# Second attention stage of a one-core graph network: the turn order of TensorE, ScalarE and VectorE rewritten

## The chip, the cores and the metric

The kernel runs on one core of one Trainium2 chip. The metric is the device time of one launch in microseconds (us); the time before is the median of three runs. A profile of one further execution was recorded.

## The reference, cut to what matters

A network of four graph layers over 100,000 nodes with 64 features and 50,000 edges, everything in float32. The change touches the second layer alone, a graph attention with four heads:

```python
h = jnp.maximum(_layernorm(x, axis=-1), 0.0)
xl = (h @ W_l + b_l).reshape(n, HEADS, C)
xr = (h @ W_r + b_r).reshape(n, HEADS, C)
e = (edge_attr @ W_e).reshape(-1, HEADS, C)
g = jax.nn.leaky_relu(xl[src] + xr[dst] + e, NEG_SLOPE)
logits = jnp.einsum('ehc,hc->eh', g, att)
amax = jax.ops.segment_max(logits, dst, num_segments=n)
ex = jnp.exp(logits - amax[dst])
denom = jax.ops.segment_sum(ex, dst, num_segments=n)
alpha = ex / (denom[dst] + 1e-16)
out = jax.ops.segment_sum(xl[src] * alpha[..., None], dst, num_segments=n).reshape(n, HEADS * C) + bias
mean, var = out.mean(axis=0), out.var(axis=0)
out = (out - mean) * jax.lax.rsqrt(var + BN_EPS) * gamma + beta
return jax.nn.gelu(out + h, approximate=False)
```

## The kernel before, in words

The kernel is a row of stages, one after the other, with a barrier between them; stage two is `conv_gatv2` (from L1366). Edges are sorted by target node and cut into 98 chunks of 512 edges. A chunk is worked on feature-major: a tile of 128 partitions by 512 columns holds the source node's 64 features in partitions 0 to 63 and the target's in 64 to 127.

Work is pipelined by hand. `slots` (L167) runs a body once per turn for every engine; in one turn the body gets the chunks k0, k1, ... k6, where k3 is the chunk that is three turns behind k0. Each engine runs the steps of its body in the order in which they are written, and semaphores tie the engines together; nothing else sets the order. The steps of one turn before the change are these.

- TensorE (body at L1543): the edge product `w_e1` into `p_g` (L1548) and the node product `w_lr` onto it (L1550), both for k3; the centering product of k2 (`norm.center`, L726); four transposes of the gathered rows of k0 (L1563); the variance product of k2 (L734); four transposes of the edge attributes of k2 (`ea.turn`, L1021); the score product of k3 (L1573); eight small products that add the finished rows of k6 to the column statistics (`stat.add`, L1046); four transposes of the running sums of k5 (L875).
- ScalarE (body at L1441): copy of the source half out of PSUM and of the position column for k1 (L1447, L1448); two activations that make `g` for k3 (L1454, L1455); the square of k2 (L730); the near exponential of k4 (L823); logarithm and exponential that make the reciprocal deviation of k2 (L741, L743); copy of the edge attributes of k2 (L1026); square of the finished rows of k6 (L1465); the far exponential of k4 (L828).
- VectorE (body at L1482): the normed and clamped tile `hT` of k3 (`norm.scale_to`, L748, a maximum with zero and a product in one instruction); the backward scan of k1 (L1494); then the softmax of k4, k5 and k6 interleaved: the denominator (L848), a carried column (L787), the scan of the sums (L837), the reciprocal (L852), the scan of the maxima (L806), the mask (L1513), near difference (L810), carried far sum (L814), quotient (L857), a copy of the mask for the statistics (L1525), far difference (L818), and last the weights (L1531).
- GpSimd gathers: per turn it copies the row numbers (L906) and issues four indirect transfers (L918), held until ScalarE's L1448 has freed a row buffer three turns on.
- SyncE issues seven transfers per turn (L1396 to L1419): target rows, a keep mask, the stores of `xT`, `hT` and the output rows, the far mask and the edge attributes; each is held by a semaphore of the step that fills or frees its buffer.

`p_cen` (the centered tile, PSUM) and the square have one buffer each, `xT` and `hT` four, `p_g` two. The edge attributes are transposed into the bank of the variance, `p_var`, so the variance product of a turn can come only when the attributes of the turn before have been copied out.

Of the kernel before, what the change touches and what calls it, by code (L numbers as in the profile page):

```python
# [31 lines left out]
P = 128  # L32
D = 64
TPC = 4
# [162 lines left out]
def hold(eng, sem, n):  # L197

    eng.wait_ge(sem, n)
    eng.nop(nofuse=True)  # L200
# [1165 lines left out]
def conv_gatv2(nc, c, dram, x1, e1, eo1, edge_attr, xs, hs):  # L1366
# [4 lines left out]
    with Scope(nc, "l1") as s:  # L1371
        rows = Rows(s, [(x1, POS + D, 0, c.idx_src)], POS + 2 * D)
        kept = Kept(s, 2 * D)
        norm = NormT(s, "n")
        sm = Softmax(s, 1)
        xT = [s.sb(f"xT{q}", [P, CE]) for q in range(4)]
        hT = [s.sb(f"hT{q}", [P, CE]) for q in range(4)]
        ea = EdgeAttr(s, edge_attr, 16, 0, norm.p_var)
        g = s.sb("g", [P, CE])
        keep = [s.sb(f"keep{u}", [P, CE]) for u in range(2)]  # L1380
        last = s.sb("last", [P, TPC])
        stat = Stats(s)
        end_rows, end_x, end_T = s.sb("end_rows", [P, POS + D]), s.sb("end_x", [P, P]), s.sb("end_T", [P, P])
        p_xT, p_score = s.ps("p_xT"), s.ps("p_score")
# [9 lines left out]
        with nc.Block() as block:  # L1394
# [40 lines left out]
            @block.scalar  # L1435
            def _(act):
                load_ln_exp(nc, act)
                act.wait_ge(end_gathered, 16)
                act.activation(c.end_pos[:], end_rows[:, 0:POS].bitcast(I32), ACT.Copy).then_inc(m["end_put"], 1)

                def body(k1, k2, k3, k4, k6):  # L1441
                    if k1:
                        if not k1.round:
                            act.wait_ge(x_saved[k1.q], 16 * k1.r)
                            act.wait_ge(norm.centered, k1.n - 4)
                        act.wait_ge(m["x_turned"], k1.n)
                        act.activation(xT[k1.q][0:D, :], p_xT[0:D, :], ACT.Copy).then_inc(m["src_out"], 1)  # L1447
                        act.activation(c.idx_pos[:, bass.ds(k1.i * TPC, TPC)].unsqueeze(2), rows.buf[k1.q][:, :, 0:POS].bitcast(I32),  # L1448
                                       ACT.Copy).then_inc(rows.rows_free, 1)
                    if k3:  # L1450
                        if not k3.start:
                            act.wait_ge(m["scored"], k3.n - 1)
                        act.wait_ge(m["g_summed"], k3.n)
                        act.activation(g[0:D, :], p_g[k3.u][0:D, :], ACT.Identity, bias=c.b_g1[0:D, 0:1])  # L1454
                        act.activation(g[D:P, :], p_g[k3.u][0:D, :], ACT.Relu, bias=c.b_g1[0:D, 0:1]).then_inc(m["g_ready"], 1)  # L1455
                    if k2:
                        norm.square(act, k2)
                    if k4:
                        sm.exp_near(act, k4.n)
                    if k2:  # L1460
                        norm.rsqrt(act, c, k2)
                        ea.copy_out(act, k2.n)
                    if k6:
                        act.wait_ge(kept.out_ready, k6.n)
                        act.activation(kept.out[k6.q][:, :, D:P], kept.out[k6.q][:, :, 0:D], ACT.Square).then_inc(m["sums_ready"], 1)  # L1465
                    if k4:
                        sm.exp_far(act, k4.n)
                slots(act, c.NCH, 6, lambda k0, k1, k2, k3, k4, k5, k6: body(k1, k2, k3, k4, k6))
                stat.scalar(act, c)

            @block.vector
            def _(dve):
# [6 lines left out]
                early(dve.tensor_copy(end_T[D:P, :], p_xT[D:P, 0:P]))  # L1479
                step = Steps(dve, m["even_step"], m["odd_step"])  # L1480

                def body(k1, k3, k4, k5, k6):  # L1482
                    if k3:
                        if not k3.round:
                            dve.wait_ge(h_saved[k3.q], 16 * k3.r)
                        if not k3.first:
                            dve.wait_ge(m["g_summed"], k3.n - 2)
                        norm.scale_to(dve, k3, hT[k3.q][:])
                    if k1:
                        if not k1.round:  # L1490
                            dve.wait_ge(x_saved[k1.q], 16 * k1.r)
# [26 lines left out]
                    if k6:  # L1518
                        if not k6.round:
                            dve.wait_ge(o_saved[k6.q], 16 * k6.r)  # L1520
                        if not k6.start:
                            dve.wait_ge(m["sums_added"], k6.n - 1)
                        step.ended(masked)
                        sm.quotient(dve, kept.out[k6.q][:, :, 0:D]).then_inc(kept.out_ready, 1)
                        dve.tensor_copy(last[:], c.last_d[:, bass.ds(k6.i * TPC, TPC)]).then_inc(m["last_ready"], 1)  # L1525
                    if k4:
                        step.ended(carried)
                        sm.shift_far(dve, k4)
                        dve.wait_ge(sm.near_exped, k4.n)
                        w = sm.weights()  # L1530
                        dve.scalar_tensor_tensor(w, p_g[k4.u][D:P, :], c.b_l1[D:P, 0:1], w, ALU.add, ALU.mult).then_inc(m["valued"], 1)  # L1531
                slots(dve, c.NCH, 6, lambda k0, k1, k2, k3, k4, k5, k6: body(k1, k3, k4, k5, k6), step)

                stat.vector(dve, c, c.gamma1, c.beta1, c.bias1, c.scale1, c.shift1, raw=True)

# [1 line left out]
            def _(pe):  # L1537
# [2 lines left out]
                pe.transpose(p_xT[:, 0:P], end_x[:], c.ident[:]).then_inc(m["end_turned"], 1)  # L1540
                hold(pe, m["early_step"], 3)

                def body(k0, k1, k2, k3, k4, k5, k6):  # L1543
                    if k3:
                        if not k3.first:
                            hold(pe, m["valued"], k3.n - 2)
                        hold(pe, ea.ready, k3.n)
                        pe.matmul(p_g[k3.u][:], c.w_e1[:].rearrange("p a f -> p (a f)"), ea.T[0][0:16, :], start=True, stop=False)  # L1548
                        hold(pe, norm.done, k3.n)
                        pe.matmul(p_g[k3.u][:], c.w_lr[:].rearrange("p a f -> p (a f)"), hT[k3.q][:], start=False, stop=True  # L1550
                                  ).then_inc(m["g_summed"], 1)
                    if k2:
                        hold(pe, m["src_out"], k2.n)
                        hold(pe, m["keep_used"], k2.n)
                        norm.center(pe, c, k2, xT[k2.q][:])
                    if k0:
                        if k1:
                            hold(pe, m["src_out"], k1.n)
# [4 lines left out]
                            ins = pe.transpose(p_xT[:, j * P:(j + 1) * P], rows.buf[k0.q][:, j, POS:POS + 2 * D], c.ident[:])  # L1563
                        ins.then_inc(m["x_turned"], 1)
                    if k2:
                        norm.variance(pe, c, k2)
                        hold(pe, norm.logged, k2.n)
                        ea.turn(pe, c, k2)
                    if k3:
                        if k4:  # L1570
                            hold(pe, sm.shifted, k4.n)
                        hold(pe, m["g_ready"], k3.n)
                        pe.matmul(p_score[:], c.w_att1[:], g[:], start=True, stop=True).then_inc(m["scored"], 1)  # L1573
                    if k6:
                        hold(pe, m["last_ready"], k6.n)
                        hold(pe, m["sums_ready"], k6.n)
                        stat.add(pe, last, kept.out[k6.q], m["sums_added"])
                    if k5:
                        if k6:
                            hold(pe, kept.out_ready, k6.n)  # L1580
                        sm.turn(pe, c, k5)
                slots(pe, c.NCH, 6, body)
                stat.finish(pe, c)


# [956 lines left out]
```

## Time and profile before

| what | value |
|---|---|
| median of three runs | 6815.02 us (6811.41 to 6820.18) |
| the profiled execution's own time | 6795.73 us |
| span of the profile | 6793.8 us |
| busy share of the span: TensorE, VectorE, ScalarE, GpSimd | 62%, 69%, 49%, 66% |
| mean granted TensorE clock | 0.895 of 2.4 GHz |
| products L1550 of stage two | from 1823.3 to 2812.0 us |

The sum of the prediction is made against the profiled execution. A timeline row gives the start, the duration, the engine (PE is TensorE, PEld its weight load, DVE VectorE, ACT ScalarE, POOL GpSimd, SPq the SyncE queue), the line, the operation and the tiles; x is the number of instructions merged into the row, and in brackets stands the idle time before it with what ended it. A row that covers two passes of one product (x2) gives them as one. Instructions of one engine can overlap by some hundredths of a microsecond, and TensorE's more, since its ends are modelled: distances from start to start are the safer reading.

### The profile page before, as it was taken

Reading aid. Unit: us, or ns where it says so; the run is one execution under the profiler, and the core shown is the slowest. Engines: PE = TensorE matmul, PEld = TensorE weight load, DVE = VectorE, ACT = ScalarE, POOL = GpSimd, SP = SyncE. Lnnn points to the kernel's source line nnn. Section 1 sums busy time; section 2 is a strip of 40 time slices with the busy share of each in tenths; the row PEclk is TensorE's granted clock in tenths of the full one; section 3 lists DMA queues with packets and bytes.
Section 4 is the critical chain, followed back from the end, with each engine's and each line's share of the span. In section 5 each row is a group of like instructions: output and inputs, shape, how many; then the busy total and the mean of one; then the engine's idle time right before and its main releaser. Section 6 shows DMA issues by size and latency. Waiting matters only on the chain. (4 is left out here: it accounts for less than half of the span.)

```text
span 6793.8 us, 85831 instructions
## 1 busy us (share of the span) xinstructions
PE 4193.3 (62%) x15111; PEld 2135.7 (31%) x15111; DVE 4701.1 (69%) x9073; ACT 3325.8 (49%) x5670; POOL 4502.1 (66%) x4877
## 2 busy tenths in 40 slices
PE   0102555555477777699996777775777677777700
PEld 0000211111133333266663333332434344444400
DVE  5885888888577777576664555555777667766667
ACT  1112444444355555487885666665777733333300
POOL 4777888888644444265546888886766477777744
PEclk9999999999999999799997888887999978778855
DMA  2442222222344444499983344443333233333377
GB/s 89 140 144 56 81 74 74 78 74 74 83 132 131 132 132 129 104 186 193 192 178 93 114 114 114 114 114 93 75 80 78 65 66 71 69 71 69 69 297 309
DMA packets 949964, 773.07 MB, mean 114 GB/s; under 512 B 661199, under 2 KB 727708, under 8 KB 945875
## 3 DMA queue, kind: packets, MB, share of 16 engines
q1 hardware_dynamic: 819859, 614.72, 30.6%
q0 software_dynamic: 125504, 131.83, 12.2%
q10 hardware_dynamic: 4512, 25.60, 0.9%
q14 instruction: 66, 0.54, 0.0%
q8 instruction: 23, 0.38, 0.0%
HBM read 472.43 MB, written 310.28 MB: 115 GB/s over the span
## 5 line engine op out<-in xcount | busy, mean ns | idle before, releaser
L205 ACT ACT_TABLE_LOAD x621 | 796.7, 1283 | 139.3 <-PEq L66 128.6
L954 POOL DMA_INDIRECT x<-l_out,l_snum x392 | 472.5, 1205 | 106.5 <-issue 90.1
L918 POOL DMA_INDIRECT l_rows<-x,l_num x392 | 441.2, 1126 | 153.5 <-issue 93.7
L954 POOL DMA_INDIRECT m<-l2s_out,l2s_snum x392 | 439.2, 1120 | 146.5 <-issue 105.7
L1159 POOL DMA_INDIRECT pre_src_rows<-in_x,all_idx_src x392 | 397.2, 1013 | 164.3 <-issue 130.0
L918 POOL DMA_INDIRECT l_rows<-in_x,l_num x392 | 432.1, 1102 | 105.7 <-issue 90.6
L918 POOL DMA_INDIRECT l3a_rows<-m,l3a_num x392 | 398.6, 1017 | 144.3 <-issue 93.3
L918 POOL DMA_INDIRECT l2s_rows<-vc_rows,l2s_num x392 | 416.5, 1062 | 106.3 <-issue 95.5
L918 POOL DMA_INDIRECT l_rows<-eo,l_num x392 | 387.5, 989 | 147.7 <-issue 96.7
L954 POOL DMA_INDIRECT xg<-l3b_out,l3b_snum x392 | 395.2, 1008 | 113.2 <-issue 90.3
L918 POOL DMA_INDIRECT l3b_rows<-g_rows,l3b_num x392 | 385.6, 984 | 106.2 <-issue 92.4
L837 DVE TENSOR_TENSOR_SCAN l2s_sums<-l2s_ex,l2s_sums 128x512 f32<-128x512 f32 x97 | 124.6, 1284 | 458.3 <-ACT l2s_ex L828 458.3
L1349 PE MATMUL l_p_hT<-all_ident,l_h 128*128 128x128 f32 x392 | 109.2, 433 | 468.5 <-DVE l_h L681 468.5
L2407 PE MATMUL l3b_p_gate<-all_w_gate,l3b_acc 128*128 128x256 f32 x784 | 305.4, 557 | 32.5 <-DVEq L2366 31.4
L310 ACT ACTIVATE prep_pay<-prep_pay 128x512 f32<-128x512 f32 x136 | 85.7, 630 | 416.9 <-DVEq L396 416.9
L734 PE MATMUL l_n_p_var<-l_n_sq,all_w_mean 128*128 128x512 f32 x392 | 220.7, 645 | 95.9 <-ACT l_n_sq L730 95.6
L2399 PE MATMUL l3b_p<-all_ident,l3b_hm 128*128 128x128 f32 x392 | 126.6, 345 | 231.0 <-DVEq L2359 231.0
L1349 PEld LDWEIGHTS l_p_hT<-all_ident,l_h 128*128 128x128 f32 x392 | 70.0, 217 | 631.6 <-DVE l_h L681 631.6
L432 PE MATMUL prep_ptk<-all_ident,prep_key 128*128 128x128 f32 x72 | 20.1, 434 | 402.2 <-DVEq L382 402.2
L1981 PE MATMUL l2s_p_score<-l2s_vT,all_w_head 68*128 68x512 f32 x196 | 110.3, 645 | 238.9 <-ACT l2s_vT L1918 238.9
L1708 DVE TENSOR_TENSOR_SCAN l_p_oT<-l_keep,l_end_T,l_p_oT 64x512 f32<-64x512 f32 x98 | 127.5, 1301 | 185.5 <-PE l_p_oT L1782 148.2
L2454 POOL TENSOR_TENSOR dl_min<-dl_min,all_shift 128x1600 f32<-128x1600 f32 x32 | 131.2, 4099 | 182.7 <-DMA dl_min<-m 182.7
(407 smaller groups left out, 13700.1 us busy)
## 6 DMA issues: line engine op xcount, KB each, us to landing
l_far<-far_d SPq DMA_DIRECT2D x196, 256.0 KB, 3.4
xg<-l2s_bg_row SPq DMA_DIRECT2D x97, 512.0 KB, 3.8
dl_xin<-xg SPq DMA_DIRECT2D x31, 1600.0 KB
l2s_bg_x<-x SPq DMA_DIRECT2D x97, 260.0 KB, 3.0
x<-ts_row SPq DMA_DIRECT2D x31, 812.5 KB, 4.4
l_keep<-keep_d SPq DMA_DIRECT2D x196, 128.0 KB, 2.9
xs<-l_xT SPq DMA_DIRECT2D x98, 256.0 KB, 2.7
hs<-l_hT SPq DMA_DIRECT2D x98, 256.0 KB, 3.0
```

Source lines behind the costliest of these rows:

```text
L205: act.add_instruction(mybir.InstLoadActFuncSet(name=nc.get_next_instruction_name(), ins=[], outs=[], act_func_set_id=which))
L734: pe.matmul(self.p_var[:], c.w_mean[:], self.sq[:], start=True, stop=True).then_inc(self.spread, 1)
L837: dve.tensor_tensor_scan(self.sums[k.u][:], self.ex[:, 0, :], self.ex[:, 1, :], 0.0 if k.start else self.sums[1 - k.u][:, CE - 1:CE], ALU. ...
L918: pool.indirect_dma_start(self.buf[k.q][:, j, at:at + w], None, table, bass.IndirectOffsetOnAxis(ap=self.num[k.q][:, m, j:j + 1], axis=0)) ...
L954: pool.indirect_dma_start(self.table, bass.IndirectOffsetOnAxis(ap=self.num[k.q][:, j:j + 1], axis=0), self.out[k.q][:, j, 0:self.cols], N ...
L1159: pool.indirect_dma_start(c.src_rows[:, t, :], None, x, bass.IndirectOffsetOnAxis(ap=c.idx_src[:, t:t + 1], axis=0)).then_inc(c.src_gather ...
L1349: ins = pe.transpose(p_hT[:, j * P:(j + 1) * P], h[:, j, :], c.ident[:])
L1708: swept = step(dve.tensor_tensor_scan(p_oT[D:P, ::-1], keep[k1.q][D:P, ::-1], p_oT[D:P, ::-1], end_T[D:P, bass.ds(k1.i, 1)], ALU.mult, ALU ...
L1981: pe.matmul(p_score[k1.u][:], c.w_head[:], vT[k1.u][:], start=True, stop=True).then_inc(m["scored"], 1)
L2399: pe.transpose(p_01[:, cols], hm[:, j, 0:P], c.ident[:])
L2407: ins = pe.matmul(p_gates[:, j, :], acc[k1.u][:, j * P:(j + 1) * P], c.w_gate[:], start=True, stop=True)
L2454: pool.tensor_tensor(min_[k.u][:], min_[k.u][:], over_rows(c.shift3[0:NP, :], NR), ALU.add).then_inc(pool_done, 1)
```

## The change

The order of a turn is rewritten on three engines. TensorE starts with the centering product of k2, then does the edge product of k3, the variance of k2, the node product of k3, the row transposes, the attribute transposes, the statistics (now of k7, one turn later, with two buffers for the mask `last`), the score and the transposes of the sums. ScalarE starts with the far exponential of the chunk whose far difference was made in the turn before (k5), and does square, logarithm and exponential of k2 ahead of `g`; the attribute copy is last. VectorE makes `hT` for k2, in the turn in which its deviation is made, in the place before the weights, and no longer for k3 at the head of the turn. Some waits move with their steps: the quotient waits for the statistics of two turns before, and `hT` for the node product of four chunks before. SyncE's and GpSimd's bodies are unchanged.

```diff
-        last = s.sb("last", [P, TPC])
+        last = [s.sb(f"last{u}", [P, TPC]) for u in range(2)]
@@ ScalarE
-                def body(k1, k2, k3, k4, k6):
+                def body(k1, k2, k3, k4, k5, k6):
+                    if k5:
+                        sm.exp_far(act, k5.n)
                     if k1:
...
+                    if k2:
+                        norm.square(act, k2)
+                        norm.rsqrt(act, c, k2)
                     if k3:
...
-                    if k2:
-                        norm.square(act, k2)
                     if k4:
                         sm.exp_near(act, k4.n)
-                    if k2:
-                        norm.rsqrt(act, c, k2)
-                        ea.copy_out(act, k2.n)
                     if k6:
...
-                    if k4:
-                        sm.exp_far(act, k4.n)
+                    if k2:
+                        ea.copy_out(act, k2.n)
@@ VectorE
-                def body(k1, k3, k4, k5, k6):
-                    if k3:
-                        if not k3.round:
-                            dve.wait_ge(h_saved[k3.q], 16 * k3.r)
-                        if not k3.first:
-                            dve.wait_ge(m["g_summed"], k3.n - 2)
-                        norm.scale_to(dve, k3, hT[k3.q][:])
+                def body(k1, k2, k4, k5, k6):
                     if k1:
...
-                        if not k6.start:
-                            dve.wait_ge(m["sums_added"], k6.n - 1)
+                        if not k6.first:
+                            dve.wait_ge(m["sums_added"], k6.n - 2)
...
                     if k4:
                         step.ended(carried)
                         sm.shift_far(dve, k4)
+                    if k2:
+                        if not k2.round:
+                            dve.wait_ge(h_saved[k2.q], 16 * k2.r)
+                            dve.wait_ge(m["g_summed"], k2.n - 4)
+                        norm.scale_to(dve, k2, hT[k2.q][:])
+                    if k4:
                         dve.wait_ge(sm.near_exped, k4.n)
@@ TensorE
-                def body(k0, k1, k2, k3, k4, k5, k6):
+                def body(k0, k1, k2, k3, k4, k5, k6, k7):
+                    if k2:
+                        hold(pe, m["src_out"], k2.n)
+                        hold(pe, m["keep_used"], k2.n)
+                        norm.center(pe, c, k2, xT[k2.q][:])
                     if k3:
...
                         pe.matmul(p_g[k3.u][:], c.w_e1[:].rearrange("p a f -> p (a f)"), ea.T[0][0:16, :], start=True, stop=False)
+                    if k2:
+                        norm.variance(pe, c, k2)
+                    if k3:
                         hold(pe, norm.done, k3.n)
...
-                    if k2:
-                        hold(pe, m["src_out"], k2.n)
-                        hold(pe, m["keep_used"], k2.n)
-                        norm.center(pe, c, k2, xT[k2.q][:])
                     if k0:
...
                     if k2:
-                        norm.variance(pe, c, k2)
                         hold(pe, norm.logged, k2.n)
                         ea.turn(pe, c, k2)
+                    if k7:
+                        hold(pe, m["last_ready"], k7.n)
+                        hold(pe, m["sums_ready"], k7.n)
+                        stat.add(pe, last[k7.u], kept.out[k7.q], m["sums_added"])
                     if k3:
...
-                    if k6:
-                        hold(pe, m["last_ready"], k6.n)
-                        hold(pe, m["sums_ready"], k6.n)
-                        stat.add(pe, last, kept.out[k6.q], m["sums_added"])
                     if k5:
...
-                slots(pe, c.NCH, 6, body)
+                slots(pe, c.NCH, 7, body)
```

## Rows read from the trace of the kernel before

**Rows 1.** Line L1550: duration min, median, max in ns, first and last start.

```profile
span 6793.8 us, 85831 instructions
...
L1550 PE MATMUL l_p_g<-l_hT,all_w_lr x196: 592/697/1222, 1823.3 to 2812.0; 128*128 128x512 f32 x196
```

**Rows 2.** One full turn of stage two, TensorE and ScalarE: the timeline.

```profile
2207.13 1.13 PE L1550 MATMUL l_p_g<-l_hT,all_w_lr 128*128 128x512 f32 x2
...
2208.35 0.68 ACT L1454 ACTIVATE l_g<-l_p_g,all_b_g 64x512 f32<-64x512 f32 x1 [2.87 <-PE l_p_g L1550]
...
2209.76 0.60 ACT L730 ACTIVATE l_n_sq<-l_n_p_cen 128x512 f32<-128x512 f32 x1
...
2210.50 1.10 PE L734 MATMUL l_n_p_var<-l_n_sq,all_w_mean 128*128 128x512 f32 x2 [0.94 <-ACT l_n_sq L730]
...
2211.69 0.69 ACT L741 ACTIVATE l_n_rstd<-l_n_p_var,all_eps 128x512 f32<-128x512 f32 x1 [0.82 <-PE l_n_p_var L734]
...
2212.63 0.60 PE L1021 MATMUL l_n_p_var<-all_ident,l_ea 128*32 128x128 f32 x4 [1.04 <-ACT l_n_rstd L741]
...
2213.26 0.59 ACT L1026 ACTIVATE l_eaT<-l_n_p_var 32x512 f32<-32x512 f32 x1 [0.22 <-PE l_n_p_var L1021]
...
2213.76 0.40 ACT L1465 ACTIVATE l_out<-l_out 128x256 f32<-128x256 f32 x1
...
2214.30 1.03 PE L1046 MATMUL l_p_stat<-l_out,l_last 128*1 128x128 f32 x8 [0.21 <-ACT l_out L1465]
...
2216.90 1.13 PE L1550 MATMUL l_p_g<-l_hT,all_w_lr 128*128 128x512 f32 x2
```

**Rows 3.** Windows: us, busy time per engine (PE, PEld, DVE, ACT, POOL), PEclk, DMA share, GB/s.

```profile
2150.00:2300.00 150.00, 118.66 (x443) 52.63 (x443) 114.03 (x204) 84.32 (x161) 68.22 (x72) 0.94 0.48 130
```

**Rows 4.** The timeline where the granted clock falls, TensorE, the turn after rows 2.

```profile
2222.49 1.01 PE L1021 MATMUL l_n_p_var<-all_ident,l_ea 128*32 128x128 f32 x4 [1.13 <-ACT l_n_rstd L741]
...
2223.30 1.92 PE L1573 MATMUL l_p_score<-l_g,all_w_att 128*128 128x512 f32 x2
...
2228.06 1.13 PE L1550 MATMUL l_p_g<-l_hT,all_w_lr 128*128 128x512 f32 x2
```

**Rows 5.** VectorE in one turn: the ends of its two unbroken stretches, and two neighbours.

```profile
2206.19 0.17 DVE L848 TENSOR_SCALAR l_rden<-l_p_sums 128x16 f32<-128x16 f32 x1 [0.97 <-PE l_p_sums L875]
...
2209.02 0.69 DVE L810 TENSOR_TENSOR l_ex<-l_p_score,l_top 128x512 f32<-128x512 f32 x1
...
2209.63 0.68 DVE L814 TENSOR_TENSOR l_ex<-l_top,l_far 128x512 f32<-128x512 f32 x1
...
2211.35 0.76 DVE L1531 SCALAR_TENSOR_TENSOR l_ex<-l_p_g,all_b_l,l_ex 64x512 f32<-64x512 f32 x1
...
2213.18 0.69 DVE L748 SCALAR_TENSOR_TENSOR l_hT<-l_n_p_cen,l_n_rstd 128x512 f32<-128x512 f32 x1 [1.08 <-ACT l_n_rstd L743]
...
2213.90 1.29 DVE L1494 TENSOR_TENSOR_SCAN l_xT<-l_keep,l_end_T,l_p_xT 64x512 f32<-64x512 f32 x1
```

**Rows 6.** The timeline: score product and sum transposes of the same turn.

```profile
2213.06 1.02 PE L1573 MATMUL l_p_score<-l_g,all_w_att 128*128 128x512 f32 x2
...
2215.26 0.66 PE L875 MATMUL l_p_sums<-all_ident,l_sums 128*128 128x128 f32 x4
```

**Rows 7.** Waits of the SyncE queue, 1900 to 2790 us: total us, times, longest us.

```profile
SPq L200 <- DVE l_ex L818: 320.3, 87, 6.8
```

**Rows 8.** GpSimd in one turn, timeline: row numbers, first and last gather.

```profile
2215.54 0.19 POOL L906 COPY l_num<-all_idx_src 128x4 int32 x1 [3.17 <-ACT all_idx_pos L1448]
...
2216.35 1.95 POOL L918 DMA_INDIRECT l_rows<-x,l_num  x1 [0.62 <-POOL l_num L906]
...
2221.20 0.94 POOL L918 DMA_INDIRECT l_rows<-x,l_num  x1 [0.30 <-issue]
```

**Rows 9.** Timeline of the stage's first turns, TensorE at the lower clock.

```profile
1821.38 2.04 PE L1548 MATMUL l_p_g<-l_eaT,all_w_e 16*128 16x512 f32 x2 [0.77 <-ACT l_eaT L1026]
1823.35 2.08 PE L1550 MATMUL l_p_g<-l_hT,all_w_lr 128*128 128x512 f32 x2
```

More of the change, by code:

```diff
@@ L1465, in body @@
                         act.activation(kept.out[k6.q][:, :, D:P], kept.out[k6.q][:, :, 0:D], ACT.Square).then_inc(m["sums_ready"], 1)
-                    if k4:
-                        sm.exp_far(act, k4.n)
-                slots(act, c.NCH, 6, lambda k0, k1, k2, k3, k4, k5, k6: body(k1, k2, k3, k4, k6))
+                    if k2:
+                        ea.copy_out(act, k2.n)
+                slots(act, c.NCH, 6, lambda k0, k1, k2, k3, k4, k5, k6: body(k1, k2, k3, k4, k5, k6))
                 stat.scalar(act, c)
@@ L1520, in body @@
                             dve.wait_ge(o_saved[k6.q], 16 * k6.r)
-                        if not k6.start:
-                            dve.wait_ge(m["sums_added"], k6.n - 1)
+                        if not k6.first:
+                            dve.wait_ge(m["sums_added"], k6.n - 2)
                         step.ended(masked)
                         sm.quotient(dve, kept.out[k6.q][:, :, 0:D]).then_inc(kept.out_ready, 1)
-                        dve.tensor_copy(last[:], c.last_d[:, bass.ds(k6.i * TPC, TPC)]).then_inc(m["last_ready"], 1)
+                        dve.tensor_copy(last[k6.u][:], c.last_d[:, bass.ds(k6.i * TPC, TPC)]).then_inc(m["last_ready"], 1)
                     if k4:
@@ L1531, in body @@
                         dve.scalar_tensor_tensor(w, p_g[k4.u][D:P, :], c.b_l1[D:P, 0:1], w, ALU.add, ALU.mult).then_inc(m["valued"], 1)
-                slots(dve, c.NCH, 6, lambda k0, k1, k2, k3, k4, k5, k6: body(k1, k3, k4, k5, k6), step)
+                slots(dve, c.NCH, 6, lambda k0, k1, k2, k3, k4, k5, k6: body(k1, k2, k4, k5, k6), step)
                 stat.vector(dve, c, c.gamma1, c.beta1, c.bias1, c.scale1, c.shift1, raw=True)
```

## The prediction, made before the changed kernel was run

> **What bounds the kernel now.** I read the stage first, then one turn of it. L1550 runs once per turn, in two passes; its 98 turns start between 1823.3 and 2812.0 us [rows 1]. So a turn takes 988.7 / 97 = 10.19 us on average, and a microsecond less per turn is worth 97 us of 6793.8.
>
> The timeline of one full turn, from L1550 to the next L1550, takes 2216.90 - 2207.13 = 9.77 us [rows 2]. Follow it by the starts. The node product hands over to `g` on ScalarE after 1.22; the two halves of `g` hold ScalarE 1.41 until the square; square to variance 0.74; variance to logarithm 1.19; logarithm to the attribute transposes 0.94; to their copy 0.63; to the square of the finished rows 0.50; to the statistics 0.54; and 2.60 of TensorE's own order (statistics, sum transposes, edge product) until the next node product. That is 9.77, the whole turn: the bound is no engine but one ring that goes three times from TensorE to ScalarE and back inside a turn. The bracketed idle times say the same: TensorE waits 0.94 for the square, 1.04 for the logarithm and 0.21 for the finished square, ScalarE 2.87 for the node product [rows 2].
>
> No engine is full. TensorE needs 9.77 - 0.94 - 1.04 - 0.21 = 7.58 us per turn [rows 2]. VectorE works in two stretches without a break: from L848 at 2206.19 to the end of the weights at 2211.35 + 0.76 = 2212.11, which is 5.92, and from L748 at 2213.18 to the end of the scan at 2213.90 + 1.29 = 2215.19, which is 2.01. Together 7.93 [rows 5].
>
> The other 0.42 us of the mean come from the clock. The window over some fifteen turns has a granted clock of 0.94 [rows 3]. In the next turn the attribute transposes take 1.01 in place of 0.60 and the score 1.92 in place of 1.02, after an idle 1.13 [rows 2, 4, 6]: 1.2 in place of 2.4 GHz. That turn takes 2228.06 - 2216.90 = 11.16, so 1.39 more [rows 2, 4]. About every third turn of the stage is like this.
>
> **The change, part by part.** No instruction is added or taken away in a turn; the statistics come one turn later, with a second `last`. All of the effect is in which wait ends last.
>
> *The ring goes.* Statistics of k7 wait for a square made a turn earlier, so their 0.21 falls away and nothing is late in their place. The node product needs an `hT` made in the turn before, so square to logarithm to `hT` to product no longer stand in one turn with `g` behind them. The attribute copy, last on ScalarE, feeds the next turn's edge product, which is second on TensorE behind the centering product.
>
> *The ring that is left.* Centering product, square, variance, logarithm, exponential, `g` twice, score, sum transposes, next centering product. Priced from rows: product to square has no row (now ScalarE is busy with `g` when it ends); the bounds are its own length of about 1.02 (the score's, same shape) [rows 6] and the 1.22 from node product to `g` [rows 2]; I take 1.22, a product handed to ScalarE. Square to variance 0.74, variance to logarithm 1.19 [rows 2]; logarithm to `hT` 2213.18 - 2211.69 = 1.49 [rows 2, 5], less a hop of 0.14 (square to variance, 0.74 less its 0.60), is 1.35 until `g`; `g` 1.41 and a hop of 0.14 [rows 2]; score 1.02 and sum transposes 0.66 [rows 6]. Sum 1.22 + 0.74 + 1.19 + 1.35 + 1.41 + 0.14 + 1.02 + 0.66 = 7.73. That is under VectorE's 7.93, by little: a hop that is 0.03 dearer at each of seven places closes the gap.
>
> *VectorE.* Its order is scan, softmax, `hT`, weights, and it never has to wait if its inputs come in time. `hT` waits for this turn's exponential: scan, softmax and far difference come first, some 6.4 us of work (7.93 less `hT` and weights), while square to exponential starts early in the turn: time to spare. Queued behind that wait are the weights and the next scan, and behind the weights TensorE's next edge product. The weights wait for the near exponential, which now stands behind both `g` on ScalarE; by the ring it ends some 0.3 us before they come. This is the wait that would bite first. The scan of the sums waits for the far exponential, now first in the same turn on ScalarE; denominator, carry and row scan (over 1.5 us) cover it. So VectorE becomes the bound, at 7.93. The ends are 7.85 (0.08 of overlap, as below, at the seam between the stretches) and 8.2 (0.3 lost at the weights); I take 8.0, the measured 7.93 with a little jitter, since no input is late by the working above.
>
> *TensorE* has 7.58 of work in 8.0; 0.4 us of idle time per turn is left, ahead of the score, where there were 2.19. The clock fell after idle times of that kind [rows 4], so I cost the lower clock at nothing; a case below takes it back.
>
> *Queues.* SyncE's and GpSimd's bodies stay, but their turns get shorter. SyncE stands 320.3 us in 87 turns, 3.7 a turn, waiting for the far difference alone [rows 7]; a turn 2.2 us shorter still leaves 1.5. `hT` is made a turn earlier per chunk, while its ring of four is stored in SyncE's old place; the overwrite comes some two turns after the store is issued. GpSimd needs 2221.20 + 0.94 - 2215.54 = 6.60 a turn and waits for ScalarE the other 3.17 [rows 8]: it fits into 8.0.
>
> *Sum.* 97 x (10.19 - 8.0) = 212 us. Against the profiled execution's own 6795.7 that is 6583; this execution lies 19 us (0.28%) under the median of the three runs, 6815.0, and against that the forecast is 6603, say 6602. Runs of this kernel differ by 0.13%, so under 0.2% (14 us) I call nothing a difference. The lower end of the turn, 7.85, saves 227 us and gives 6588, and the last three turns, which have no backward scan (3 x 1.29) [rows 5], some 4 less.
>
> **A rule weighed.** The far sum starts at 2209.63 while the near difference of 2209.02 + 0.69 still has 0.08 to go [rows 5]; so VectorE's turn is the distance of its starts, and 7.93 holds. The Trainium skill, page "VectorE: DVE Perf Modes", section "The DRAIN you can't avoid", says that the next operation is not issued until the pipe of the last is empty; by it a turn would be the plain sum of the durations, about that of rival 2. The trace disagrees with the strict reading, by the 0.08.
>
> **The rivals.**
> 1. *The clock keeps falling* every third turn, though TensorE is busier. Each time costs 1.39 less the 0.4 of slack: 1.0 / 3 x 97 = 32 us, 6635. For it: the falls come with TensorE already busy 118.66 of 150 us [rows 3]. Against: idle time shrinks from 2.19 to 0.4. Chance 0.13.
> 2. *VectorE's turn is longer*: at new seams (`hT` to weights to scan) or all along, no overlap. With the 0.08 lost at half of its fourteen instructions (the short ones show none), the turn is 7.93 + 0.56 = 8.5: 97 x 1.69 = 164 us, 6651. Against: the stretch of 5.92 is already measured with its overlaps. Chance 0.07.
> 3. *GpSimd becomes the bound.* The first gather takes 1.95, the last 0.94 [rows 8]: the first begins beside the scan of the sums. Were two more lengthened by 1.0, its turn would be 8.6: 97 x 1.59 = 154 us, 6661. Against: its 6.6 us already span the scan and both far differences, the same work it will meet. Chance 0.04. The Trainium skill, page "SBUF — State Buffer", section "SBUF: two separate sides", has a port pair that VectorE and GpSimd take from each other for whole instructions; no row here shows more than the one long gather.
> 4. *No gain*: a wait that I took for covered closes a ring near 10.2 again, and the change does not do what it says; 6815. The weights would have to come 2.2 us late. Chance 0.03.
> 5. *Slower*: the granted clock stays at the lower level through the stage. In the first turns the node product takes 2.08 [rows 9] and not 1.13 [rows 2], 1.84 times as long; a turn of TensorE is then 7.58 x 1.84 = 13.9, and 97 x 3.7 = 360 us are lost, 7175. It decides from the point at which TensorE needs over 10.19, with 41% of its work at the lower level. Against: 0.94 granted now [rows 3]. Chance 0.03.
>
> **How the numbers follow.** The forecast, VectorE-bound near 8.0 a turn, has the remaining 0.70 and sets the time, 6602. Its own spread is 6575 to 6625 (7.85 a turn and the last turns, 6584, less 9 for the spread of the runs; 8.2 a turn). The range takes in rivals 1 to 3: 6575 to 6661. Left out are rivals 4 and 5 and the tails of the first, under 0.2 in all. Faster: 0.70 + 0.13 + 0.07 + 0.04 = 0.94; same 0.03; slower 0.03.
>
> **What would show it.** Right: L1550's first and last start some 775 us apart; no idle time before the variance product that the square ended beyond some tenths; no idle time of VectorE over 0.1 us per turn; an attribute transpose always at 0.60 and a granted clock near 1.0. Step by step: weights that wait for L823 mean that `g` ahead of the near exponential was the price; TensorE idle ahead of the score and ended by L1455 means the ring of 7.73 was dearer than priced; idle time ahead of L848 ended by the sum transposes means TensorE's own order is the bound. Wrong: a turn over 9 us at full clock, or L1573 at 1.92 in most turns.

## The result, and the profile after

The changed kernel takes 6559.7 us (median of four runs, 6558.7 to 6561.4) where the kernel before takes 6813.2 in the same comparison: a ratio of 0.9627, 95% interval 0.9610 to 0.9643, 253.5 us less. The forecast was 6602 with a range of 6575 to 6661, so the direction and most of the size were right and the time lies 15 us under the range. The profiled execution of the changed kernel took 6559.05 us by itself, that of the kernel before 6795.73: 236.7 less.

The line that answers to [rows 1], with the duration's minimum, median and maximum in ns and the first and last start:

```profile
span 6557.2 us, 85933 instructions
...
L1557 PE MATMUL l_p_g<-l_hT,all_w_lr x196: 592/592/1062, 1826.0 to 2577.4; 128*128 128x512 f32 x196
```

97 turns now take 2577.4 - 1826.0 = 751.4 us, 7.75 each where it was 10.19. That is 237.3 us less, as much as the spans of the two profiles differ (6793.8 - 6557.2 = 236.6): nearly all of the difference of the profiles is stage two's turn. The window that answers to [rows 3]:

```profile
2150.00:2300.00 150.00, 139.03 (x577) 66.71 (x576) 148.10 (x270) 108.55 (x211) 92.88 (x97) 1.00 0.67 174
```

VectorE is busy 148.1 of 150 us, up from 114.0; the granted clock is 1.00, up from 0.94. One turn of the timeline, from backward scan to backward scan, shows who waits:

```profile
2202.58 1.28 DVE L1488 TENSOR_TENSOR_SCAN l_xT<-l_keep,l_end_T,l_p_xT 64x512 f32<-64x512 f32 x1
...
2203.86 0.60 ACT L730 ACTIVATE l_n_sq<-l_n_p_cen 128x512 f32<-128x512 f32 x1 [0.44 <-PE l_n_p_cen L726]
2203.89 0.17 DVE L848 TENSOR_SCALAR l_rden<-l_p_sums 128x16 f32<-128x16 f32 x1
...
2204.17 1.27 DVE L837 TENSOR_TENSOR_SCAN l_sums<-l_ex,l_sums 128x512 f32<-128x512 f32 x1
...
2205.36 0.23 DVE L852 RECIPROCAL l_rden<-l_rden 128x16 f32<-128x16 f32 x1
...
2206.03 0.69 ACT L741 ACTIVATE l_n_rstd<-l_n_p_var,all_eps 128x512 f32<-128x512 f32 x1 [1.57 <-PE l_n_p_var L734]
...
2208.34 0.69 DVE L818 TENSOR_TENSOR l_ex<-l_ex,l_top 128x512 f32<-128x512 f32 x1
2208.66 0.63 ACT L823 ACTIVATE l_ex<-l_ex 128x512 f32<-128x512 f32 x1
2208.94 0.69 DVE L748 SCALAR_TENSOR_TENSOR l_hT<-l_n_p_cen,l_n_rstd 128x512 f32<-128x512 f32 x1
...
2209.28 1.10 PE L1579 MATMUL l_p_score<-l_g,all_w_att 128*128 128x512 f32 x2 [0.65 <-DVE l_ex L818]
...
2209.66 0.76 DVE L1531 SCALAR_TENSOR_TENSOR l_ex<-l_p_g,all_b_l,l_ex 64x512 f32<-64x512 f32 x1
...
2210.33 1.28 DVE L1488 TENSOR_TENSOR_SCAN l_xT<-l_keep,l_end_T,l_p_xT 64x512 f32<-64x512 f32 x1
```

No VectorE row has idle time in brackets: its 2210.33 - 2202.58 = 7.75 us are the turn. TensorE waits in one place only, 0.65 ahead of the score, and for VectorE's far difference (L818). ScalarE waits 1.57 and 0.44 for TensorE's products; VectorE, which sets the turn, does not wait for either. The near exponential (L823) ends at 2209.29, 0.37 before the weights (L1531) start.

### The profile page after: what moved, and what is told of

Same layout as the page of the kernel before. It is cut to its first block and busy times, and to the rows that moved or that the text cites. A ratio compares the mean times of both kernels' runs of the same rounds, so it can differ in the third digit from the quotient of the medians.

```text
span 6557.2 us, 85933 instructions
## 1 busy us (share of the span) xinstructions
PE 4111.0 (63%) x15111; PEld 2125.2 (32%) x15111; DVE 4689.3 (72%) x9073; ACT 3313.6 (51%) x5670; POOL 4496.8 (69%) x4877
## 5 line engine op out<-in xcount | busy, mean ns | idle before, releaser
L837 DVE TENSOR_TENSOR_SCAN l2s_sums<-l2s_ex,l2s_sums 128x512 f32<-128x512 f32 x97 | 124.6, 1285 | 463.1 <-ACT l2s_ex L828 463.1
L837 DVE TENSOR_TENSOR_SCAN l_sums<-l_ex,l_sums 128x512 f32<-128x512 f32 x194 | 248.3, 1280 | 3.5
```

The costliest lines, as they stand in the source:

```text
L837: dve.tensor_tensor_scan(self.sums[k.u][:], self.ex[:, 0, :], self.ex[:, 1, :], 0.0 if k.start else self.sums[1 - k.u][:, CE - 1:CE], ALU. ...
```

## The experiments

Theory A is that VectorE's own order now bounds the turn, with a ring between TensorE and ScalarE a little under it, and that before the bound was the ring alone. The rivals are named in the expectations. The runs were made in three groups, on the chips numbered 7, 4 and 7 again, and the kernel before was timed with each: 6826.3, 6821.3 and 6800.2 us. Stage three takes 673 to 710 us in the traces, by the execution (last group below), so besides the ratio to the kernel before of its own group each run is read by its own turn: last less first start of the node product, over 97. The changed kernel's own ratio was 0.9627 first and 0.9650 in its repeat, 16 us apart, so comparisons of ratios between groups are no finer than that.

**The statistics back in the old place (undoing one part).**

```diff
-                    if k7:
-                        hold(pe, m["last_ready"], k7.n)
...
                         pe.matmul(p_score[:], c.w_att1[:], g[:], start=True, stop=True).then_inc(m["scored"], 1)
+                    if k6:
+                        hold(pe, m["last_ready"], k6.n)
+                        hold(pe, m["sums_ready"], k6.n)
+                        stat.add(pe, last[k6.u], kept.out[k6.q], m["sums_added"])
```

> Changed kernel with the statistics back on k6 and back behind the score product. Theory A (the turn of 7.75 us is VectorE's own order; behind it stands a ring of product, square, variance, logarithm, exponential, g, score, sum transposes with about 0.5 us to spare, read from the end of g to the score): the statistics, 0.96, now stand inside that ring, 7.25 + 0.96 = 8.2 a turn, 97 x 0.46 = 45 us more than the changed kernel, 6605. Rival B (the statistics cost only the 0.21 us for which TensorE waited before): at most 20 us more, 6560 to 6580.

Measured: ratio 0.9742 (0.9721 to 0.9762), so 0.0115 of the time, some 78 us, is lost against the changed kernel's first ratio. The node product's line, and the timeline of a turn:

```profile
L1557 PE MATMUL l_p_g<-l_hT,all_w_lr x196: 592/592/697, 1821.0 to 2638.4; 128*128 128x512 f32 x196
...
2202.06 1.10 PE L1575 MATMUL l_p_score<-l_g,all_w_att 128*128 128x512 f32 x2 [1.09 <-ACT l_g L1460]
...
2203.09 1.03 PE L1046 MATMUL l_p_stat<-l_out,l_last 128*1 128x128 f32 x8
...
2204.06 0.66 PE L875 MATMUL l_p_sums<-all_ident,l_sums 128*128 128x128 f32 x4
...
2204.55 1.02 PE L726 MATMUL l_n_p_cen<-l_xT,all_w_center 128*128 128x512 f32 x2
...
2205.50 1.12 PE L1552 MATMUL l_p_g<-l_eaT,all_w_e 16*128 16x512 f32 x2
...
2205.61 0.60 ACT L730 ACTIVATE l_n_sq<-l_n_p_cen 128x512 f32<-128x512 f32 x1 [1.16 <-PE l_n_p_cen L726]
...
2206.55 1.12 PE L734 MATMUL l_n_p_var<-l_n_sq,all_w_mean 128*128 128x512 f32 x2
...
2207.78 0.69 ACT L741 ACTIVATE l_n_rstd<-l_n_p_var,all_eps 128x512 f32<-128x512 f32 x1 [1.57 <-PE l_n_p_var L734]
...
2209.03 0.67 ACT L1459 ACTIVATE l_g<-l_p_g,all_b_g 64x512 f32<-64x512 f32 x1
```

The turn is (2638.4 - 1821.0) / 97 = 8.43 us, 0.22 above the expected 8.2, and 97 x (8.43 - 7.75) = 66 us lost in it; the score now waits 1.09 for `g` and no longer for VectorE. The mechanism is theory A's ring but for one step: score to statistics to sum transposes to centering product to edge product to variance to logarithm to `g` and back to the score. The square ends at 2205.61 + 0.60 = 2206.21, and the variance starts 0.34 later, without idle time ahead of it, behind the edge product (L1552): from centering product to variance it is TensorE's own order that takes 2.00, and the square stands beside the ring. Rival B's 20 us fall short by a factor of three to four. The same rows give an estimate of the ring that the changed kernel has left: 8.43 less the 0.97 from the start of the statistics to the start of the sum transposes is 7.46.

**`hT` back at the head of VectorE's turn (undoing another part).**

```diff
+                    if k3:
...
+                        if not k3.first:
+                            dve.wait_ge(m["g_summed"], k3.n - 2)
+                        norm.scale_to(dve, k3, hT[k3.q][:])
                     if k1:
...
-                    if k2:
...
-                        norm.scale_to(dve, k2, hT[k2.q][:])
```

> Changed kernel with hT back at the head of VectorE's turn, for k3; TensorE and ScalarE keep the new order. Theory A: VectorE's turn holds the same fourteen instructions, only the seams change by up to 0.1 us, and the next centering product comes about 0.5 us later, inside the slack of the ring: 0 to 15 us more, 6560 to 6575. Rival C (the gain comes from hT being made a turn earlier): most of it is lost, over 6700.

Measured: ratio 0.9704 (0.9688 to 0.9719), 52 us lost; the turn is (2630.6 - 1830.4) / 97 = 8.25.

```profile
L1558 PE MATMUL l_p_g<-l_hT,all_w_lr x196: 592/592/1061, 1830.4 to 2630.6; 128*128 128x512 f32 x196
...
2200.65 1.10 PE L726 MATMUL l_n_p_cen<-l_xT,all_w_center 128*128 128x512 f32 x2 [0.20 <-DVE l_hT L748]
...
2206.59 0.63 ACT L823 ACTIVATE l_ex<-l_ex 128x512 f32<-128x512 f32 x1
...
2207.25 0.76 DVE L1532 SCALAR_TENSOR_TENSOR l_ex<-l_p_g,all_b_l,l_ex 64x512 f32<-64x512 f32 x1 [0.28 <-ACT l_ex L823]
...
2208.04 0.69 DVE L748 SCALAR_TENSOR_TENSOR l_hT<-l_n_p_cen,l_n_rstd 128x512 f32<-128x512 f32 x1
```

Neither expectation fits. At the head of the turn `hT` comes right behind the weights of the turn before, and a new ring closes: the centering product waits until `hT` has read the one buffer of the centered tile, `hT` comes after the weights, the weights wait 0.28 for the near exponential, and that stands behind variance, logarithm, exponential and `g`, which follow the centering product. I had counted the 0.5 us by which the product comes later against the slack ahead of the score, and overlooked the 0.37 ahead of the weights. So `hT` in front of the weights is worth half a microsecond a turn in the new order.

**A second far sum on VectorE, in both kernels.**

```diff
+                        dve.tensor_tensor(spare[:], sm.top[k4.u][:, 0:CE], sm.far[k4.u][:], ALU.add)
                         carried = step(sm.carry_far(dve, k4))
```

> Changed kernel with the far sum made a second time on VectorE, into a spare tile (0.60 us from start to start). Theory A (VectorE's order is the bound): 97 x 0.60 = 58 us more, 6618. Rival D (TensorE's order or the ring through ScalarE is the bound and VectorE is only nearly full): under 20 us more.

> Kernel before with the same second far sum. Theory A (before, the turn is a ring between TensorE and ScalarE, and VectorE idles 1.85 us in it): nothing, 6813 within 10 us. Rival D' (VectorE's far difference holds the score product back): up to 58 us more, 6871.

In the changed kernel, the node product's line and the score's:

```profile
L1558 PE MATMUL l_p_g<-l_hT,all_w_lr x196: 592/592/697, 1820.6 to 2626.6; 128*128 128x512 f32 x196
...
2206.81 1.10 PE L1580 MATMUL l_p_score<-l_g,all_w_att 128*128 128x512 f32 x2 [1.15 <-DVE l_ex L818]
```

In the kernel before, its line:

```profile
L1551 PE MATMUL l_p_g<-l_hT,all_w_lr x196: 592/697/1222, 1819.7 to 2809.4; 128*128 128x512 f32 x196
```

The same instruction costs (2626.6 - 1820.6) / 97 = 8.31 less 7.75, 0.56 us a turn, after the change (ratio 0.9738, 0.9721 to 0.9755) and nothing before it (10.20 a turn, ratio 0.9995, 0.9986 to 1.0005). The bound has moved to VectorE, and TensorE's wait ahead of the score grew by the same half microsecond. The time lost against the changed kernel's first ratio, 0.0111 or 76 us, is 22 more than 97 x 0.56 = 54. Stage three has the rest in the profiles: its projections start from 2691.3 to 3396.5 here, 705.2 us, and from 2640.6 to 3324.2 in the changed kernel's first profile, 683.6.

**More work on TensorE, in both kernels.** Four more transposes ahead of the attribute transposes in the changed kernel:

```diff
                         hold(pe, norm.logged, k2.n)
+                        for j in range(TPC):
+                            pe.transpose(ea.p[0:32, j * P:(j + 1) * P], c.ident[:, 0:32], c.ident[:])
                         ea.turn(pe, c, k2)
```

> Changed kernel with four more transposes on TensorE right ahead of the attribute transposes (about 0.43 us from start to start). Theory A (VectorE bounds the turn; TensorE idles 0.55 to 0.65 us ahead of the score): hidden, 6560 within 6 us. Rival D (TensorE's order is the bound): 97 x 0.43 = 42 us more, 6602.

```profile
L1557 PE MATMUL l_p_g<-l_hT,all_w_lr x196: 592/592/697, 1821.8 to 2572.3; 128*128 128x512 f32 x196
```

The turn stays at 750.5 / 97 = 7.74; the ratio, 0.9641 (0.9625 to 0.9658), agrees with the changed kernel's, though its 6577.0 us on that chip are not within 6 of 6560. TensorE has room, VectorE has none: rival D falls. In the kernel before, the idle time was filled:

```diff
                     if k2:
+                        for _ in range(5):
+                            pe.transpose(stat.p[:, 3 * P:4 * P], c.ident[:], c.ident[:])
                         norm.variance(pe, c, k2)
+                        for _ in range(5):
+                            pe.transpose(stat.p[:, 3 * P:4 * P], c.ident[:], c.ident[:])
                         hold(pe, norm.logged, k2.n)
```

> Kernel before with ten transposes of a constant per turn on TensorE, into a part of a bank that nobody reads, five in the idle time ahead of the variance and five in that ahead of the attribute transposes (about 0.14 us each). If the clock falls because TensorE idles 2.2 us a turn: granted clock near 1.0 in stage two, the longer third turn gone, 97 x 0.42 = 41 us less than before, 6772. If the falls have another cause: no gain, 6813, or somewhat more if the fill is late into the ring.

This fill shares its bank with the column statistics and spoils their sum, so it serves as an experiment only; order and amount of the other work are those of the kernel before. Node product, attribute transposes and window:

```profile
L1550 PE MATMUL l_p_g<-l_hT,all_w_lr x196: 592/645/697, 1824.8 to 2771.4; 128*128 128x512 f32 x196
...
L1021 PE MATMUL l_n_p_var<-all_ident,l_ea x392: 269/271/273, 1822.4 to 2766.9; 128*32 128x128 f32 x196
...
2150.00:2300.00 150.00, 132.73 (x615) 69.90 (x614) 119.38 (x214) 88.09 (x169) 72.50 (x77) 1.00 0.52 136
```

The granted clock is 1.00 and the turn 946.6 / 97 = 9.76, the full-clock turn of [rows 2]; no attribute transpose takes over 273 ns, where the longest took 421 in the kernel before. The ratio is 0.9942 (0.9926 to 0.9959), 40 us less, as expected: with TensorE's idle time filled the clock no longer falls, and that is worth 97 x 0.43 = 42 us of the whole gain.

**Each part alone, in the kernel before.** The statistics one turn later:

```diff
+                    if k7:
+                        hold(pe, m["last_ready"], k7.n)
+                        hold(pe, m["sums_ready"], k7.n)
+                        stat.add(pe, last[k7.u], kept.out[k7.q], m["sums_added"])
                     if k3:
                         if k4:
...
-                        stat.add(pe, last, kept.out[k6.q], m["sums_added"])
```

> Kernel before with one part of the change alone: the statistics one turn later (k7, ahead of the score, two buffers for the mask). Theory A (the ring of 9.77 us): attribute copy, finished square and the wait for it leave the ring, which runs 1.22 + 1.41 + 0.74 + 1.19 + 0.94 and then only through TensorE's own order (0.43 + 0.96 + 0.95 + 0.59 + 1.05): 9.48, so 97 x 0.29 = 28 us less than before, a tenth of the whole gain; ratio near 0.996. Rival E (the statistics are the main thing): over 100 us less.

```profile
L1550 PE MATMUL l_p_g<-l_hT,all_w_lr x196: 592/697/1222, 1815.5 to 2805.5; 128*128 128x512 f32 x196
...
2200.21 1.12 PE L1550 MATMUL l_p_g<-l_hT,all_w_lr 128*128 128x512 f32 x2
...
2209.74 1.13 PE L1550 MATMUL l_p_g<-l_hT,all_w_lr 128*128 128x512 f32 x2
...
2215.34 0.68 PE L1021 MATMUL l_n_p_var<-all_ident,l_ea 128*32 128x128 f32 x4 [1.14 <-ACT l_n_rstd L741]
...
2215.96 1.86 PE L1046 MATMUL l_p_stat<-l_out,l_last 128*1 128x128 f32 x8
...
2217.75 1.80 PE L1577 MATMUL l_p_score<-l_g,all_w_att 128*128 128x512 f32 x2
...
2220.97 1.13 PE L1550 MATMUL l_p_g<-l_hT,all_w_lr 128*128 128x512 f32 x2
```

The full-clock turn is 2209.74 - 2200.21 = 9.53, near the expected 9.48, but the next one takes 2220.97 - 2209.74 = 11.23 with statistics and score at a granted clock of 0.50, and over the stage 41 of the 97 turns take over 10.4 us where it was 32: 990.0 / 97 = 10.21 a turn, no gain, where 28 us were expected. The ratio, 0.9987 (0.9977 to 0.9997), is about an eighth of a percent off 1. The clock took back what the ring had won. `hT` early:

```diff
-                    if k3:
...
-                        norm.scale_to(dve, k3, hT[k3.q][:])
...
                         sm.shift_far(dve, k4)
+                    if k2:
...
+                        norm.scale_to(dve, k2, hT[k2.q][:])
+                    if k4:
                         dve.wait_ge(sm.near_exped, k4.n)
```

> Kernel before with another part alone: hT made for k2 on VectorE ahead of the weights, one turn earlier; ScalarE and TensorE in their old order. Theory A: the ring of before runs from the node product through g, square, variance and logarithm, and hT does not stand in it: nothing, 6815 to 6825, ratio 1.000 within 0.002. Rival C (hT a turn earlier is the main thing): over 100 us less.

```profile
L1550 PE MATMUL l_p_g<-l_hT,all_w_lr x196: 592/645/697, 1822.1 to 2808.3; 128*128 128x512 f32 x196
```

986.2 / 97 = 10.17 a turn, ratio 1.0004 (0.9994 to 1.0015): nothing, as expected. Alone neither part pays; in the new order the one is worth 0.68 us a turn (8.43 to 7.75) and the other 0.50. With either of them undone, 1.76 or 1.94 of the 2.44 us a turn are still there: the rest of the new order, on TensorE and ScalarE, carries the larger part, and no run takes that away by itself.

**Less work on VectorE, and both kernels once more.** The carried column and the mask copy go to ScalarE, and the reciprocal reads the denominator where it lies:

```diff
-                        bottom = step(sm.bottom(dve, k6.n))
...
-                        brought = sm.carry(dve, step, k4)
...
-                        inverse = step(sm.invert(dve))
+                        dve.wait_ge(sm.sums_turned, k6.n)
+                        inverse = step(dve.reciprocal(sm.rden[:], ...))
...
-                        dve.tensor_copy(last[k6.u][:], c.last_d[:, bass.ds(k6.i * TPC, TPC)]).then_inc(m["last_ready"], 1)
@@ ScalarE
+                        act.activation(sm.top[k4.u][:, 0:1], sm.top[1 - k4.u][:, CE:CE + 1], ACT.Copy).then_inc(m["top_carried"], 1)
...
+                        act.activation(last[k6.u][:], c.last_d[:, bass.ds(k6.i * TPC, TPC)], ACT.Copy).then_inc(m["last_ready"], 1)
```

> Changed kernel with less on VectorE: the carried column and the copy of the mask go to ScalarE, and the reciprocal reads the denominator directly (the sum with 1e-16, which leaves a float32 of 1 or more as it is, is left out). Theory A: VectorE's turn is 0.20 + 0.07 + 0.07 = 0.34 shorter, to 7.4 where the ring takes over: 97 x 0.3 = 29 us less than the changed kernel, 6531. Rival D: no gain, 6560.

> Kernel before, unchanged, timed and profiled once more. The profiled execution was 17 to 19 us faster than the median of its runs, and the forecast carried that distance over. If the distance belongs to the execution that was profiled: a new profile lies elsewhere, and ratio 1. If it belongs to the kernel (a profile always runs faster here): again some 6796 beside a median of 6813.

> The changed kernel once more, on the chip of the next run. Theory A and the rivals: stage two as in its first profile, 799 us from the first to the last product of the statistics' sum; the time itself follows stage three on this chip, 6560 to 6590.

> The leaner form of the changed kernel (carried column and mask copy on ScalarE, reciprocal straight from the denominator) beside the changed kernel on one chip. Theory A: its first profile had a turn of 7.57 in place of 7.75 us, so 97 x 0.18 = 17 us less than the run before this one, in its time too. Rival: stage two gains and stage three, bound by its transfers, takes it back: no difference.

The leaner kernel first took 6566.0 us, a ratio of 0.9623 (0.9606 to 0.9640), which is not apart from the changed kernel's first 0.9627: the expected 29 us did not come. Side by side in the last group it takes 6538.8 us (ratio 0.9619, 0.9606 to 0.9632) and the changed kernel 6552.0 (0.9650, 0.9637 to 0.9664): 13 us less, about 0.2 to 0.3%, intervals apart, where 17 were expected. The two profiled executions do not show it (6548.8 and 6546.2): there stage three took 693.1 us in the leaner kernel (2620.0 to 3313.1) and 673.1 in the changed one, which is the rival's case. In the leaner kernel's second run, the node product and a stretch of VectorE:

```profile
L1558 PE MATMUL l_p_g<-l_hT,all_w_lr x196: 592/592/1061, 1822.9 to 2557.2; 128*128 128x512 f32 x196
...
2206.08 1.28 DVE L1492 TENSOR_TENSOR_SCAN l_xT<-l_keep,l_end_T,l_p_xT 64x512 f32<-64x512 f32 x1
2207.39 1.28 DVE L837 TENSOR_TENSOR_SCAN l_sums<-l_ex,l_sums 128x512 f32<-128x512 f32 x1
2208.71 0.26 DVE L1501 RECIPROCAL l_rden<-l_p_sums 128x16 f32<-128x16 f32 x1
2208.88 1.19 DVE L806 TENSOR_TENSOR_SCAN l_top<-l_far,l_top,l_p_score 128x512 f32<-128x512 f32 x1
```

The turn is 734.3 / 97 = 7.57, 0.18 shorter and not 0.34. VectorE is still without a gap: the reciprocal starts 1.32 after the scan of the sums, behind its end, where it started 1.19 after it, within it, in the changed kernel (L837 and L852 in the result's timeline); that is 0.13 of the missing 0.16. The Trainium skill, page "VectorE: DVE Perf Modes", section "Two Vector instructions with no wait between them", says that an instruction whose operand starts in another quarter of the partitions than the last one read from that memory is held until all earlier ones have ended. The rows agree: the last read from PSUM was the backward scan's, in the upper half of the partitions, and the reciprocal's is in the lower.

For the repeats of the kernel before and the changed kernel, the first and last projection of stage three, whose code is the same in all. The kernel before, profiled again:

```profile
L1747 PE MATMUL l_p_qkv<-all_w_qkv,l_hT x784: 272/275/582, 2880.2 to 3588.4; 128*128 128x128 f32 x196
...
3100.00:3300.00 200.00, 189.06 (x886) 125.34 (x884) 136.16 (x220) 158.32 (x220) 115.32 (x140) 0.94 0.98 186
```

In its first profile:

```profile
L1747 PE MATMUL l_p_qkv<-all_w_qkv,l_hT x784: 272/275/582, 2882.6 to 3563.7; 128*128 128x128 f32 x196
```

The changed kernel in its repeat:

```profile
L1749 PE MATMUL l_p_qkv<-all_w_qkv,l_hT x784: 272/275/583, 2640.0 to 3313.1; 128*128 128x128 f32 x196
```

Stage three, with its DMA engines busy 0.98 of the time, took 708.2 us in the second profile of the kernel before, 681.1 in the first and 673.1 in the changed kernel's repeat. The second profile's span is 6821.9, 28.1 longer than the first's, and 27.1 of that is stage three. This time the profiled execution (6823.9) lay 4 us over the median of its runs (6819.9), so the distance belongs to the execution that was profiled, and not to the kernel. The changed kernel's repeat has stage two as before, 751 us from the first to the last node product, and its 6552.0 us lie under the 6560 to 6590 that were expected; against the kernel before of its group that is 248 us less.

## Why the prediction was wrong, and where it was right

It forecast 212 us less and got 253.5. Two steps of the sum make up the 41.5, but for the rounding; the mechanism, VectorE's order as the bound, was right.

*The size of VectorE's turn.* "VectorE becomes the bound, at 7.93 ... I take 8.0": the bound is right, the number is not. It measured 7.75, and 97 x (8.0 - 7.746) = 24.6 us. I had summed two stretches by their outer ends and then added jitter. Two seams of the new order are cheaper. Far difference to `hT` is 2208.94 - 2208.34 = 0.60, where far difference to weights was 2211.35 - 2210.63 = 0.72 ([rows 5] and the row below, from the same turn of the kernel before); weights to scan is 2210.33 - 2209.66 = 0.67, where the weights were counted to their end with 0.76.

```profile
2210.63 0.69 DVE L818 TENSOR_TENSOR l_ex<-l_ex,l_top 128x512 f32<-128x512 f32 x1
```

The new turn is thus 7.93 - 7.75 = 0.18 under the sum, of which the lower end, 7.85, had priced 0.08 and the forecast nothing. The 0.07 of jitter hardly came: most turns inside the stage take 7.75 and about every fourth 7.85, 7.78 in the mean. The last 0.03 are short turns at the ends of the stage, some 3 us, which the prediction had seen ("some 4 less") and left out of its 6602.

*The step from the profiled execution to the median.* The sum was made against 6795.7, 19 us under the median, and the distance was carried over to the changed kernel. It measured 6559.05 in the profile and 6559.7 in the median: no distance. That is 16.8 us more of gain, and it is not the change's. The repeat of the kernel before shows stage three spreading by that much between executions; that it was stage three here too is likely and not shown, since the other executions of the first comparison have no trace. Each step alone would have left the time inside the range, and with the ratio of the changed kernel's repeat, 0.9650, the time would have been 6815.0 x 0.9650 = 6576.5, just inside. So how far under 6602 the time fell is in part chance, and the turn is not: it is 7.74 in the repeat.

Point by point: the ring of 9.77 as the bound before was right (a second far sum costs nothing there; each part alone brings nothing or next to it). The clock at full rate was right, and so was its price: 0.42 foreseen, 0.43 by the filled kernel. The ring that is left was priced 7.73 and is 7.46 by the estimate above, and one of its steps was wrong: it was led through the square, 1.22 + 0.74 = 1.96 from centering product to variance, where the rows go through the edge product, 2.00. That the two are so near is luck. The ring is shorter because the sum transposes lead to the centering product in 2204.55 - 2204.06 = 0.49 and not 0.66, logarithm to `g` is 2209.03 - 2207.78 = 1.25 and not 1.35, and `g` to score, what is left of 8.43, 1.46 and not 1.55. The weights were named as the wait that bites first; they have 0.37 to spare in the changed kernel, and they do wait where the statistics go back or `hT` does. Of the rivals none came: the clock stayed up, VectorE's seams were shorter and not longer, and GpSimd and SyncE stayed out of the way. From 1850 to 2570 us GpSimd still waits 126.7 us in 87 turns for a freed buffer, 1.46 a turn, and SyncE 231.6 us in 93 for the far difference, 2.5 a turn, more than the 1.5 that the prediction left it.

```profile
POOL l_num L906 <- ACT all_idx_pos L1450: 126.7, 87, 2.6
...
SPq L200 <- DVE l_ex L818: 231.6, 93, 4.8
```

Rival 5 took the first turns' node product, 2.08 us, for the lower clock [rows 9]. The duration is that of the lower clock, but the granted clock of the profile does not say so: in a window over that product it is 1.00, where it is 0.50 in a window over the slow score of [rows 4].

```profile
1823.00:1826.00 3.00, 3.00 (x4) 1.18 (x4) 0.00 (x0) 0.54 (x1) 2.22 (x5) 1.00 0.80 210
2224.00:2225.00 1.00, 1.00 (x2) 0.00 (x0) 0.93 (x1) 1.00 (x4) 0.00 (x0) 0.50 0.17 18
```

What stays open: what the new order of TensorE and ScalarE is worth without the two parts that were undone; how far VectorE could be relieved before the ring holds the turn, by the estimate of 7.46 some 0.11 under the leaner kernel; and why the products of the first turns are slow at a granted clock of 1.00.

## What to carry to other kernels

When no engine is full, look for a ring: follow the starts, at each step to what ended last, a semaphore or the engine's own queue, until the chain comes back to its own instruction, and price a reordering by the longest ring that is left and by the fullest engine's starts, whichever is larger. Price seams from start to start, and ask of each instruction that is moved which ring its new neighbours close. Parts of such a reordering can be worth nothing one by one, so test them by taking one away from the whole as well as by adding one to the old.

## What the runs showed of the hardware that was not expected

A shorter turn with less idle time saw the clock fall more often: before, TensorE stopped for 0.94, 1.04 and 0.21 us in a turn of 9.77; with the statistics moved alone it stopped for 0.95 and 1.03 in one of 9.53, and 41 turns were slow where it had been 32. The sum of the idle time alone does not say how often the clock falls, and what does is not shown. One stop of 1.09 us in a turn of 8.43 left the clock at 1.00 in the window from 2150 to 2300, as did one of 1.15 in a turn of 8.31. Ten transposes of a constant that nobody needs bought 40 us.
